# A DLRM tower on one Trainium2 core: the order and the banks of the last round's layers

## Chip, cores and metric

The kernel runs on one core of a Trainium2 (trn2) chip. The metric is the device time of one execution in microseconds; the time of a kernel is the median of its runs.

## What is computed

For each of 2048 batch rows, 26 embedding rows of 128 floats are fetched from 26 tables (1000 to 125000 rows each) by `ids`. Together with the dense vector they are 27 vectors; the 351 products of pairs of them, and the dense vector twice, go through three layers:

```python
combined = jnp.concatenate([dense_features[:, None, :], sparse_features], axis=1)
interactions = jnp.einsum('bnd,bmd->bnm', combined, combined)
interactions_flat = interactions[:, _TRIU_I, _TRIU_J]
z = jnp.concatenate([dense_features, interactions_flat], axis=1)
h = jnp.concatenate([z, r_dense_features], axis=1)
h = jnp.maximum(h @ W_top1 + b_top1, 0.0)      # 607 -> 512
h = jnp.maximum(h @ W_top2 + b_top2, 0.0)      # 512 -> 256
y = h @ W_top3                                 # 256 -> 1
```

All data are 32-bit floats.

## The kernel before

The batch is cut into eight rounds of R = 256 rows. Two rounds are one pass `i`; a round has two tiles of 128 rows, so a pass has tiles v = 0 to 3. The text calls the two rounds of the last pass (r = 0 and 1) its older and its last half.

**Where the vectors come from.** Nine small tables are kept in SBUF in a high and a low part (t_hi, t_lo), and their rows are fetched by products with a one-hot matrix that DVE makes (`fetch`, L477, and `compare`, L763). The other 17 tables are gathered from HBM by POOL, one indirect DMA for each table and tile (`gather_tile`, L402), with a clear of unread memory between two gathers (`pause`, L391). The gathered rows of a tile and its dense rows lie in `rows`, in five groups of 4, 4, 4, 4 and 2. PE transposes a group when its gathers have landed (`transpose_rows`, L437), and ACT and DVE copy the groups by turns into `vecs` (`copy_vecs`, L604).

**Products of pairs.** `dots` (L461) multiplies the vectors of two batch rows with themselves, 32 matmuls for 64 rows and a call; one call fills the two banks of `dots_ps`, the last call of the kernel those of `late_ps` (`last_dots_ps`). ACT copies a part of each block into `inter` (`take_products`, L648, 16 copies), and DVE merges the other part in with a mask (`merge_products`, L811, 16 merges). A tile has two such calls, so 32 copies and 32 merges.

**Input of layer 1.** `x_hi` and `x_lo` hold five slots of 128 inputs: four of products of pairs (JG = 4) and, as the fifth, the dense vector. ACT rounds `vecs` (L653) and `inter` (L657) into x_hi, and DVE subtracts for x_lo (L820, L823). This is `split_input`.

**Layers.** `layer1` (L500) makes M1 = 4 blocks of 128 outputs for the 256 rows of a round, in two banks by turns (mlp_ps[m % 2]). Each block takes 15 products: w_hi by x_hi and w_lo by x_hi for the five slots, then w_hi by x_lo. ACT adds the bias and rectifies a block (`rectify1`, L664), which frees its bank. `layer2` (L509) has M2 = 2 blocks of four products, each issued as two instructions, and starts when all four blocks of layer 1 are rectified. `rectify2` (L671) waits for both blocks. `layer3` (L516) has two products, also two instructions each, and starts when both are rectified. DVE copies the result out (`keep_y`, L831), and SP writes it to HBM (`write_y`, L346).

**The order of the work.** Every engine's order is written out by hand in `step` and `last_step`. In all rounds but the last, layers of one round run between fetches of the next. `last_step(i)` has no next round. On PE it is:

```python
transpose_rows(i, 3, (2,))
layer2(i, 0, 0)
stay_busy(row_ps, 14)
transpose_rows(i, 3, (3,))
layer2(i, 0, 1)
stay_busy(row_ps, 4)
transpose_rows(i, 3, (4,))
dots(i, 3, 0)
dots(i, 3, 1, last_dots_ps)
layer3(i, 0)
stay_busy(turn_ps[1], 20)
layer1(i, 1, *range(M1))      # then layer2(i, 1, 0), layer2(i, 1, 1), layer3(i, 1)
```

`stay_busy(bank, n)` (L523) issues n transposes of the identity into a bank that nobody reads: the unread products. ACT's `last_step` ends with take_products for tile 3, split_input(i, 3), four rectify1 and two rectify2; DVE's with merge_products for tile 3, keep_y(i, 0), split_input(i, 3) and keep_y(i, 1). `turn_ps` are three banks that groups and fetched items use by turns (`taken` tells when a turn's bank has been copied out); its first is the second bank of late_ps.

Of the kernel before, what the change touches and what calls it, by code (L numbers as in the profile page):

```python
# [5 lines left out]
P = 128  # L6
# [12 lines left out]
def dlrm_tower(nc, dense, ids, ids_by_round, tables, w1, w1_laid, w2, small_laid, out):  # L19
# [52 lines left out]
    with ExitStack() as ctx:  # L72
# [81 lines left out]
        mlp_ps = [ps(f"mlp_ps{m}", [P, 512])[:, 0:R] for m in range(2)]  # L154

# [266 lines left out]
        def _(pe):  # L422
# [96 lines left out]

            def stay_busy(bank, n):  # L520

                for _ in range(n):
                    pe.transpose(bank[:, 0:P], ident[:], ident[:])  # L523
# [49 lines left out]
            def last_step(i):  # L573
# [10 lines left out]
                stay_busy(row_ps, 14)  # L584
# [7 lines left out]

                stay_busy(turn_ps[1], 20)
                layer1(i, 1, *range(M1))
                layer2(i, 1, 0)
                layer2(i, 1, 1)
                layer3(i, 1)
# [22 lines left out]
        def _(act):  # L620
# [30 lines left out]
            def split_input(i, v):  # L651
                mine = slice((v % 2) * P, (v % 2 + 1) * P)
                nc.scalar.copy(x_hi[:, JG, mine].rearrange("p (h two s) -> p h two s", two=2, s=QS),  # L653
                               in_turn(vecs[v // 2][:, v % 2, :, 0])).then_inc(x_hi_made, 1)
                act.wait_ge(inter_by_act, i * (4 * NA) + (v + 1) * NA)
                act.wait_ge(inter_by_dve, i * (4 * ND) + (v + 1) * ND)
                nc.scalar.copy(x_hi[:, 0:JG, mine], inter[:]).then_inc(x_hi_made, 1)  # L657
# [69 lines left out]
            def last_step(i):  # L727
# [7 lines left out]
                split_input(i, 2)  # L735
                take_vectors(i, 3, 3)
# [3 lines left out]
                split_input(i, 3)  # L740
                rectify1(i, 1, *range(M1))
                rectify2(i, 1, 0, 1)
# [4 lines left out]
        def _(dve):  # L747
# [68 lines left out]
            def split_input(i, v):  # L816
# [4 lines left out]
                                  ALU.subtract).then_inc(x_lo_made, 1)  # L821
                dve.wait_ge(x_hi_made, i * 8 + v * 2 + 2)
# [3 lines left out]
            def keep_y(i, r):  # L826
# [4 lines left out]
                dve.tensor_copy(in_turn(y_sb[:, r, :]),  # L831
                                mlp_ps[0][0:1].rearrange("p (h two s) -> p h two s", two=2, s=QS)).then_inc(y_kept, 1)
# [52 lines left out]
            def last_step(i):  # L885
# [4 lines left out]
                split_input(i, 2)  # L890
                take_vectors(i, 3, 4)
# [3 lines left out]
                split_input(i, 3)  # L895
                keep_y(i, 1)
# [64 lines left out]
```

## Time and profile before

| | us |
|---|---|
| median of 3 runs | 477.35 (477.17 to 479.39) |
| profiled execution | 478.75 |
| its span, first to last instruction | 477.0 |
| mean granted clock of TensorE, share of full | 0.953 |
| PE busy | 417.5 |
| POOL busy | 399.8 |
| DVE busy | 338.8 |
| ACT busy | 215.8 |

PE is TensorE, PEld its weight loads, DVE VectorE, ACT ScalarE, POOL GpSimd, SP the engine that issues plain DMAs. Busy times overlap, so they don't add up to the span. A granted clock of 1.00 is the upper level of TensorE's clock (2.4 GHz), 0.50 the lower (1.2 GHz). All times in the rows are counted from the start of the span; a start together with a duration and a count (x14) is a run of like instructions that follow one another, the duration that of the whole run. Successive products overlap by their drain, so the end of one lies behind the start of the next.

### The profile page before, as it was taken

Reading aid. Unit: us, or ns where it says so; the run is one execution under the profiler, and the core shown is the slowest. Engines: PE = TensorE matmul, PEld = TensorE weight load, DVE = VectorE, ACT = ScalarE, POOL = GpSimd, SP = SyncE. Lnnn points to the kernel's source line nnn. Section 1 sums busy time; section 2 is a strip of 40 time slices with the busy share of each in tenths; the row PEclk is TensorE's granted clock in tenths of the full one; section 3 lists DMA queues with packets and bytes.
Section 4 is the critical chain, followed back from the end, with each engine's and each line's share of the span. In section 5 each row is a group of like instructions: output and inputs, shape, how many; then the busy total and the mean of one; then the engine's idle time right before and its main releaser. Section 6 shows DMA issues by size and latency. Waiting matters only on the chain.

```text
span 477.0 us, 11689 instructions
## 1 busy us (share of the span) xinstructions
PE 417.5 (88%) x4198; PEld 393.0 (82%) x4198; DVE 338.8 (71%) x777; ACT 215.8 (45%) x719; POOL 399.8 (84%) x553
## 2 busy tenths in 40 slices
PE   0546796979999999999999959999699969999796
PEld 0446696979999999899999959999698969899685
DVE  3659869798598769886897648875587848855060
ACT  1054254454545545545553624554254453545251
POOL 7999989989899898898998989989898988989300
PEclk9958788899999999999999979999899998999899
DMA  7973422622132222123223313222222213131000
GB/s 182 232 199 106 113 51 76 166 70 80 47 84 53 72 73 78 47 74 81 56 64 76 81 39 85 55 78 63 46 78 74 83 39 85 40 78 39 23 2 0
DMA packets 19682, 36.58 MB, mean 77 GB/s; under 512 B 7823, under 2 KB 10391, under 8 KB 19630
## 3 DMA queue, kind: packets, MB, share of 16 engines
q0 software_dynamic: 8704, 17.84, 16.6%
q1 hardware_dynamic: 10926, 18.04, 13.0%
q8 instruction: 33, 0.54, 0.5%
q14 instruction: 19, 0.16, 0.1%
HBM read 35.85 MB, written 0.01 MB: 75 GB/s over the span
## 4 chain that ended last, share of the span: by engine, by line
POOL 64%; issue 27%; PE 4%; ACT 2%; POOLq 1%; DMA 1%; DVE 0%; ACTq 0%; DVEq 0%
POOL rows L402 36%; POOL y_wide L391 28%; PE mlp_ps L500 2%; PE mlp_ps L509 1%; ACT inter L648 1%; POOLq L390 1%; DMA rows<-in_tbl,idx_sb 1%; PE dots_ps L461 0%; DVE inter L811 0%; DMA idx_sb<-in_ids 0%; PE mlp_ps L516 0%; PE late_ps L437 0%; ACT x_hi L657 0%; ACT h_sb L664 0%; ACT h_sb L671 0%
## 5 line engine op out<-in xcount | busy, mean ns | idle before, releaser
L402 POOL DMA_INDIRECT rows<-in_tbl,idx_sb x272 | 265.8, 977 | 45.6 <-POOL y_wide L391 43.8
L763 DVE TENSOR_TENSOR onehot<-ids_sb,late_ps 125x1024 fp32r<-125x1024 int32 (+2 forms) x154 | 167.8, 1142 | 12.6 <-DMA ids_sb<-in_ids_by_round 6.4
L811 DVE COPY_PREDICATED inter<-mask,dots_ps 27x48 f32<-27x48 int32 x496 | 103.1, 208 | 60.4 <-ACT inter L648 45.7
L391 POOL MEMSET y_wide<- 64x448 f32 x272 | 133.8, 492 | 0.2
L648 ACT COPY inter<-dots_ps 27x64 f32<-27x64 f32 x496 | 99.0, 200 | 59.1 <-PE dots_ps L461 47.8
L461 PE MATMUL dots_ps<-vecs 128*64 128x54 f32 x1984 | 118.7, 226 | 1.5 <-ACT vecs L624 0.9
L461 PEld LDWEIGHTS dots_ps<-vecs 128*64 128x64 f32 x1984 | 114.7, 140 | 6.0 <-issue 2.4
L477 PE MATMUL turn_ps<-onehot,t_hi 125*128 125x256 f32 x378 | 101.1, 304 | 10.3 <-DVE vecs L604 10.3
L477 PE MATMUL turn_ps<-onehot,t_lo 125*128 125x256 f32 x378 | 96.5, 291 | 0.0
L477 PEld LDWEIGHTS turn_ps<-onehot,t_hi 125*128 125x128 f32 x378 | 75.8, 200 | 14.8 <-issue 8.5
L477 PE MATMUL late_ps<-onehot,t_hi 125*128 125x256 f32 x214 | 59.7, 312 | 21.1 <-DVE t_lo L776 16.6
L477 PEld LDWEIGHTS turn_ps<-onehot,t_lo 125*128 125x128 f32 x378 | 76.0, 201 | 0.2
L477 PEld LDWEIGHTS late_ps<-onehot,t_hi 125*128 125x128 f32 x214 | 44.5, 208 | 24.4 <-DVE t_lo L776 18.8
L624 ACT COPY vecs<-turn_ps 128x256 f32<-128x256 f32 x46 | 28.2, 613 | 71.0 <-PE turn_ps L477 69.8
L477 PE MATMUL late_ps<-onehot,t_lo 125*128 125x256 f32 x214 | 56.5, 298 | 0.0
L477 PEld LDWEIGHTS late_ps<-onehot,t_lo 125*128 125x128 f32 x214 | 44.5, 208 | 0.1
L437 PE MATMUL turn_ps<-ident,rows 128*128 128x128 f32 x200 | 30.5, 282 | 13.3 <-DMA rows<-in_tbl,idx_sb 7.6
L500 PE MATMUL mlp_ps<-x_hi,w_hi 128*128 128x256 f32 x160 | 41.0, 291 | 1.2 <-ACT x_hi L657 1.2
L500 PE MATMUL mlp_ps<-x_hi,w_lo 128*128 128x256 f32 x160 | 39.6, 282 | 0.0
L604 DVE COPY vecs<-turn_ps 128x512 f32<-128x512 f32 (+1 forms) x28 | 17.9, 639 | 30.0 <-PE turn_ps L437 29.9
L437 PEld LDWEIGHTS turn_ps<-ident,rows 128*128 128x128 f32 x200 | 22.7, 143 | 15.9 <-DMA rows<-in_tbl,idx_sb 9.1
L624 ACT COPY vecs<-late_ps 128x256 f32<-128x256 f32 x26 | 16.0, 616 | 38.5 <-PE late_ps L477 38.0
(52 smaller groups left out, 353.3 us busy)
## 6 DMA issues: line engine op xcount, KB each, us to landing
ids_sb<-in_ids_by_round SPq DMA_DIRECT2D x25, 375.0 KB
rows<-in_tbl,idx_sb POOLq DMA_INDIRECT x272, 2.6
vecs<-in_tbl SPq DMA_DIRECT2D x8, 448.0 KB
rows<-in_r_dense_features SPq DMA_DIRECT2D x16, 64.0 KB, 5.2
h_sb<-in_W_top_laid SPq DMA_DIRECT2D x2, 512.0 KB, 18.3
vecs<-in_tbl SPq DMA_DIRECT2D x1, 560.0 KB
w_sb<-in_W_top SPq DMA_DIRECT2D x1, 512.0 KB
vecs<-in_tbl SPq DMA_DIRECT2D x8, 52.0 KB
```

What stands on the lines that cost most here:

```text
L390: pool.sem_inc(pauses_begun, 1)
L391: pool.memset(unread, 0.0).then_inc(pauses_made, 1)
L402: nc.gpsimd.indirect_dma_start(out=rows[v % 2][:, s, :], out_offset=None, in_=tables[f - 1][:, :], in_offset=bass.IndirectOffsetOnAxis(ap= ...
L437: last = pe.transpose(bank[:, n * P:(n + 1) * P], rows[u][:, s, :], ident[:])
L461: last = pe.matmul(place[h * 64:h * 64 + 64, n, 0:PAIR], vs[:, b:b + 2, :].rearrange("p b f -> p (b f)"), vs[:, b:b + 2, 0:N], start=True, ...
L477: last = pe.matmul(bank, part[0:KP, T0[k] + t, :], part_buffer(k, h)[0:KP, t - a, :], start=(t == 0 and part is t_hi), stop=(t == KT[k] - ...
L500: last = pe.matmul(mlp_ps[m % 2], w[:, jj, m * P:(m + 1) * P], x[:, jj, :], start=(at == 0), stop=(at == 3 * (JG + 1) - 1))
L604: copy(vecs[v // 2][:, v % 2, :, a:a + n], bank_of("rows", i * 4 + v, k)[:, 0:n * P].rearrange("p (f b) -> p b f", f=n)).then_inc(done, 1)
L624: nc.scalar.copy(vecs[(r + 1) % 2][:, :, :, NR + k], bank_of("item", i * 2 + r + 1, k)[:, 0:R].rearrange("p (t b) -> p t b", t=2)).then_in ...
L648: nc.scalar.copy(inter_of(u, q, g, 0, count[g]), products_of(q, g * JG, count[g], place)).then_inc(inter_by_act, 1)
L763: dve.tensor_tensor(part_buffer(k, h)[0:KP, 0:n], home.rearrange("p (o r) -> p o r", o=1).to_broadcast([KP, n, R]), row_of[KT[k]][0:KP, a: ...
L811: dve.copy_predicated(inter_of(u, q, g, a, n), mask[g * 32:g * 32 + N, a:a + n].rearrange("p (j s) -> p j s", s=1).to_broadcast([N, n, QS] ...
```

## The change

The last round's end is rewritten; all other rounds stay as they are.

- PE, ahead of the fourth group of tile 3: 32 unread products for 14.
- ACT and DVE: `split_input` is cut in two. The part for the dense vector of tile 3 (`split_dense`) is issued right after the split of tile 2, on ACT behind a wait for the copy of that tile's first group; the part for the products of pairs stays where it was.
- PE: `end_of_layers` takes the place of the 20 unread products, layer1, layer2 and layer3 of the last half. Layer 1 has a bank for each of its four blocks: two of turn_ps and the two of dots_ps, which are free once the merges of the first call of tile 3 are done. The three dense products of each block come first, then 14 unread products, then the 12 others of each block.
- PE, layer 2: first the products of both blocks with the first three parts of h1, then those with the fourth. Each product waits for its own ReLU. Each block reports by itself.
- ACT: each block of layer 2 is rectified when it is done, into another buffer (in `rows`). Layer 3's products wait for one block each, and its result goes into the first of the four banks.

```diff
+        flat_dots_ps = dots_ps[:].rearrange("p s c -> p (s c)")
+        end_ps = [turn_ps[1][:, 0:R], turn_ps[2][:, 0:R], flat_dots_ps[:, 0:R], flat_dots_ps[:, 512:512 + R]]
+        end_h2_sb = rows[0][:, 0:M2 * R // D, :].rearrange("p s d -> p (s d)").rearrange("p (m r) -> p m r", r=R)
...
+            def end_of_layers(i):
+                parts, before = i * 8 + 8, i * (2 * M1) + M1
+                pe.wait_ge(x_hi_made, parts - 1)
+                pe.wait_ge(x_lo_made, parts - 1)
+                pe.wait_ge(inter_by_act, i * (4 * NA) + 3 * NA + PER_UNIT)
+                pe.wait_ge(inter_by_dve, i * (4 * ND) + 3 * ND + PER_UNIT)
+                for m in range(M1):
+                    for n, (w, x) in enumerate(((w_hi, x_hi), (w_lo, x_hi), (w_hi, x_lo))):
+                        pe.matmul(end_ps[m], w[:, JG, m * P:(m + 1) * P], x[:, JG, :], start=(n == 0), stop=False)
+                stay_busy(mlp_ps[1], 14)
+                for m in range(M1):
+                    for at in range(3 * JG):
+                        if at < 2 * JG:
+                            jj, w, x = at // 2, (w_hi, w_lo)[at % 2], x_hi
+                        else:
+                            jj, w, x = at - 2 * JG, w_hi, x_lo
+                        if m == 0 and at == 0:
+                            pe.wait_ge(x_hi_made, parts)
+                        if m == 0 and at == 2 * JG:
+                            pe.wait_ge(x_lo_made, parts)
+                        last = pe.matmul(end_ps[m], w[:, jj, m * P:(m + 1) * P], x[:, jj, :],
+                                         start=False, stop=(at == 3 * JG - 1))
+                    last.then_inc(h1_done, 1)
+                pe.wait_ge(y_kept, i * 2 + 1)
+                for ks in (range(M1 - 1), (M1 - 1,)):
+                    for m in range(M2):
+                        for k in ks:
+                            pe.wait_ge(relu1_done, before + k + 1)
+                            last = pe.matmul(mlp_ps[m], w2_sb[:, k, m * P:(m + 1) * P], h1_sb[:, k, :],
+                                             start=(k == 0), stop=(k == M1 - 1))
+                        if M1 - 1 in ks:
+                            last.then_inc(h2_done, 1)
+                for k in range(M2):
+                    pe.wait_ge(relu2_done, i * (2 * M2) + M2 + k + 1)
+                    last = pe.matmul(end_ps[0][0:1], w3_sb[:, k:k + 1], end_h2_sb[:, k, :],
+                                     start=(k == 0), stop=(k == M2 - 1))
+                last.then_inc(y_done, 1)
...
-                stay_busy(row_ps, 14)
+                stay_busy(row_ps, 32)
...
-                stay_busy(turn_ps[1], 20)
-                layer1(i, 1, *range(M1))
-                layer2(i, 1, 0)
-                layer2(i, 1, 1)
-                layer3(i, 1)
+                end_of_layers(i)
...
                 split_input(i, 2)
+
+                act.wait_ge(*taken(turn_of["rows", i * 4 + 3, 0]))
+                split_dense(i, 3)
                 take_vectors(i, 3, 3)
                 rectify2(i, 0, 0, 1)
                 take_products(i, 3, 0)
                 take_products(i, 3, 1, last_dots_ps)
-                split_input(i, 3)
-                rectify1(i, 1, *range(M1))
-                rectify2(i, 1, 0, 1)
+                split_input(i, 3, False)
+                for m in range(M1):
+                    act.wait_ge(h1_done, i * (2 * M1) + M1 + m + 1)
+                    nc.scalar.activation(h1_sb[:, m, :], end_ps[m], ACT.Relu, bias=b1_sb[:, m:m + 1]).then_inc(relu1_done, 1)
+                for m in range(M2):
+                    act.wait_ge(h2_done, i * (2 * M2) + M2 + m + 1)
+                    nc.scalar.activation(end_h2_sb[:, m, :], mlp_ps[m], ACT.Relu,
+                                         bias=b2_sb[:, m:m + 1]).then_inc(relu2_done, 1)
...
                 split_input(i, 2)
+                split_dense(i, 3)
                 take_vectors(i, 3, 4)
                 merge_products(i, 3, 0)
                 merge_products(i, 3, 1, last_dots_ps)
                 keep_y(i, 0)
-                split_input(i, 3)
-                keep_y(i, 1)
+                split_input(i, 3, False)
+                keep_y(i, 1, end_ps[0])
```

## Rows read from the trace of the kernel before

**Rows 1.** The page: busy time by engine, and the chain that ended last.

```profile
PE 417.5 (88%) x4198; PEld 393.0 (82%) x4198; DVE 338.8 (71%) x777; ACT 215.8 (45%) x719; POOL 399.8 (84%) x553
...
POOL 64%; issue 27%; PE 4%; ACT 2%; POOLq 1%; DMA 1%; DVE 0%; ACTq 0%; DVEq 0%
```

**Rows 2.** Chain of waits near its end: start, us, what.

```profile
441.70 2.56 DMA rows<-in_tbl,idx_sb
```

**Rows 3.** PE's timeline: start, us, line, operation, count, [idle before <-releaser].

```profile
438.32 1.89 PE L509 MATMUL mlp_ps<-h_sb,w_sb 128*128 128x256 f32 x8
440.05 1.69 PE L523 MATMUL late_ps<-ident 128*128 128x128 f32 x14
444.31 0.97 PE L437 MATMUL late_ps<-ident,rows 128*128 128x128 f32 x4 [2.57 <-DMA rows<-in_tbl,idx_sb]
445.08 3.30 PE L509 MATMUL mlp_ps<-h_sb,w_sb 128*128 128x256 f32 x8
...
448.65 0.38 PE L437 MATMUL turn_ps<-ident,rows 128*128 128x128 f32 x2
...
457.56 2.40 PE L523 MATMUL turn_ps<-ident 128*128 128x128 f32 x20
461.15 0.35 PE L500 MATMUL mlp_ps<-x_hi,w_hi 128*128 128x256 f32 x1 [1.18 <-ACT x_hi L657]
...
467.81 0.76 PE L500 MATMUL mlp_ps<-x_lo,w_hi 128*128 128x256 f32 x5
469.23 3.69 PE L509 MATMUL mlp_ps<-h_sb,w_sb 128*128 128x256 f32 x16 [0.66 <-ACT h_sb L664]
473.85 1.02 PE L516 MATMUL mlp_ps<-h_sb,small 128*1 128x256 f32 x4 [0.93 <-ACT h_sb L671]
```

**Rows 4.** POOL's last gather (start, us); landing times of gathers, 438 to 450 us.

```profile
444.92 0.95 POOL L402 DMA_INDIRECT rows<-in_tbl,idx_sb  x1 [0.16 <-POOL y_wide L391]
...
DMA to landing us min/median/max: 2.5/2.5/2.6
```

**Rows 5.** Busy by engine; last three columns: granted clock, DMA share, GB/s.

```profile
440.00:444.31 4.31, 1.74 (x15) 1.45 (x14) 0.23 (x1) 0.00 (x0) 3.90 (x6) 1.00 0.17 46
444.31:448.00 3.69, 3.69 (x12) 3.12 (x13) 0.00 (x0) 0.59 (x1) 1.88 (x3) 0.54 0.14 36
457.56:461.15 3.59, 2.41 (x22) 2.20 (x21) 3.18 (x15) 2.22 (x8) 0.00 (x0) 1.00 0.00 0
```

**Rows 6.** ACT's timeline.

```profile
445.32 0.59 ACT L604 COPY vecs<-late_ps 128x512 f32<-128x512 f32 x1 [6.45 <-PE late_ps L437]
...
458.89 0.42 ACT L653 CAST x_hi<-vecs 128x128 fp32r<-128x128 f32 x1
460.43 0.62 ACT L657 CAST x_hi<-inter 128x512 fp32r<-128x512 f32 x1 [1.12 <-DVE inter L811]
...
468.61 0.47 ACT L664 ACTIVATE h_sb<-mlp_ps,small 128x256 f32<-128x256 f32 x1 [1.32 <-PE mlp_ps L500]
472.96 0.84 ACT L671 ACTIVATE h_sb<-mlp_ps,small 128x256 f32<-128x256 f32 x2 [3.88 <-PE mlp_ps L509]
```

**Rows 7.** DVE's timeline.

```profile
449.07 0.42 DVE L604 COPY vecs<-turn_ps 128x256 f32<-128x256 f32 x1 [8.84 <-PE turn_ps L437]
...
456.55 3.79 DVE L811 COPY_PREDICATED inter<-mask,late_ps 27x48 f32<-27x48 int32 x16
460.37 0.41 DVE L831 COPY y_wide<-mlp_ps 1x256 f32<-1x256 f32 x1
...
461.10 0.68 DVE L823 TENSOR_TENSOR x_lo<-inter,x_hi 128x512 fp32r<-128x512 f32 x1
```

**Rows 8.** 64 small products on PE, early and late; 56 to 62.4 us as rows 5.

```profile
58.99 5.16 PE L461 MATMUL dots_ps<-vecs 128*64 128x54 f32 x64 [0.90 <-ACT vecs L624]
...
430.96 3.75 PE L461 MATMUL dots_ps<-vecs 128*64 128x54 f32 x64
...
56.00:62.40 6.40, 5.50 (x47) 5.24 (x47) 4.01 (x4) 1.91 (x2) 5.75 (x9) 0.51 0.33 97
```

More of the change, by code:

```diff
@@ L154, in dlrm_tower @@
         mlp_ps = [ps(f"mlp_ps{m}", [P, 512])[:, 0:R] for m in range(2)]
+        flat_dots_ps = dots_ps[:].rearrange("p s c -> p (s c)")
+        end_ps = [turn_ps[1][:, 0:R], turn_ps[2][:, 0:R], flat_dots_ps[:, 0:R], flat_dots_ps[:, 512:512 + R]]
+        assert M1 == len(end_ps)
+        end_h2_sb = rows[0][:, 0:M2 * R // D, :].rearrange("p s d -> p (s d)").rearrange("p (m r) -> p m r", r=R)
         ident_set = sem("ident_set")
@@ L649, in take_products, with split_dense @@
                                        products_of(q, g * JG, count[g], place)).then_inc(inter_by_act, 1)
-            def split_input(i, v):
+            def split_dense(i, v):
                 mine = slice((v % 2) * P, (v % 2 + 1) * P)
@@ L654, in split_input @@
                                in_turn(vecs[v // 2][:, v % 2, :, 0])).then_inc(x_hi_made, 1)
+            def split_input(i, v, dense_too=True):
+                mine = slice((v % 2) * P, (v % 2 + 1) * P)
+                if dense_too:
+                    split_dense(i, v)
                 act.wait_ge(inter_by_act, i * (4 * NA) + (v + 1) * NA)
@@ L814, in merge_products, with split_dense @@
                             products_of(q, c + SECOND, n, place)).then_inc(inter_by_dve, 1)
-            def split_input(i, v):
+            def split_dense(i, v):
                 mine = slice((v % 2) * P, (v % 2 + 1) * P)
@@ L821, in split_input @@
                                   ALU.subtract).then_inc(x_lo_made, 1)
+            def split_input(i, v, dense_too=True):
+                mine = slice((v % 2) * P, (v % 2 + 1) * P)
+                if dense_too:
+                    split_dense(i, v)
                 dve.wait_ge(x_hi_made, i * 8 + v * 2 + 2)
@@ L824, in split_input, with keep_y @@
                                   ALU.subtract).then_inc(x_lo_made, 1)
-            def keep_y(i, r):
+            def keep_y(i, r, bank=mlp_ps[0]):
                 dve.wait_ge(y_done, i * 2 + r + 1)
@@ L831, in keep_y @@
                 dve.tensor_copy(in_turn(y_sb[:, r, :]),
-                                mlp_ps[0][0:1].rearrange("p (h two s) -> p h two s", two=2, s=QS)).then_inc(y_kept, 1)
+                                bank[0:1].rearrange("p (h two s) -> p h two s", two=2, s=QS)).then_inc(y_kept, 1)
             def step(now, prev):
```

## The prediction

> **What bounds the kernel now.** I read the page's shares and chain first, then the chain of waits from 430 us on, then the timelines of PE, ACT and DVE over the same stretch, and the granted clock in chosen windows. PE is busy 88% of the span and POOL 84%, yet the chain that ended last is 64% POOL: its gathers and the clears between them set the pace of everything up to the last rows [rows 1]. The change touches only what comes after, so the pace of POOL stays as it is, and the question is what the stretch from 440 us to the end is made of.
>
> That stretch has three pieces. First the last two groups of rows. The fourth group of the last tile lands at 441.70 + 2.56 = 444.26 us and is transposed at 444.31; behind it PE runs one block of layer 2 of the older half, 3.30 us, and only then the fifth group, at 448.65 [rows 2, 3]. But the last gather was issued at 444.92 and gathers take 2.5 to 2.6 us to land [rows 4]: its rows were there at about 447.52, and PE was 1.13 us late for them. It was late because of the clock. The eight products of layer 2 take 3.30 us there and 1.89 us at 438.32 [rows 3]; the mean granted clock of 444.31 to 448.00 is 0.54 of full, which is the lower level (1.2 GHz) for nearly all of it, against 1.00 up to 444.31 [rows 5]. Before the fall PE had idled 2.57 us behind 14 unread products.
>
> Second, the products and their merging, 449.59 to 461.05: 128 small products, 32 copies by ACT, 32 merges by DVE, and the cast x_hi at 460.43. DVE's last 16 merges begin at 456.55 and end at 460.34, and the cast starts at once behind them [rows 6, 7]. PE waits here; the change leaves the length of this piece alone.
>
> Third, the last half's layers on PE: 60 products of layer 1 from 461.15 to 468.57, 0.66 us idle for the last ReLU, 16 instructions of layer 2 (eight products of two each) for 3.69 us, 0.93 us idle for the two ReLUs, and 1.02 us of layer 3 [rows 3]. PE is the bound wherever it isn't waiting for ACT.
>
> **The change, part by part.**
>
> *32 unread products for 14.* Six more cost 2.40 - 1.69 = 0.71 us (20 against 14), 0.118 us each [rows 3]; 18 more end at 440.05 + 1.69 + 18 x 0.118 = 443.86 us. The rows land at 444.27, so nothing waits for them, with 0.4 us to spare, and PE's idle stretch falls from 2.57 to some 0.45 us. What does this do to the clock? No row shows 32 of them, so both ends: nothing (the fall comes as before), or no fall. The nearest row is 457.56 to 461.15: 20 unread products and then 1.18 us of idle, and the clock stays at 1.00 through it and behind it [rows 5]. I take no fall. Then layer 2 starts at about 444.8 and needs 1.89 us, the four unread products 0.45 more: PE is through at about 447.2, before the rows at 447.52. The fifth group is transposed at 447.52 in place of 448.65: **1.13 us**, and DVE's copy (449.07), the products and all that follows come as much earlier. DVE waits there for PE [rows 7], and ACT's ReLUs of that half are done by 447.6 (446.7 + 0.04 + 0.84), ahead of its next work. The upper end is also 1.13, since the gather sets it; the lower is 0.
>
> The Trainium skill says otherwise ("TensorE: Matmul & The Clock Gate", Part 4: PE-mode transpose): work in transpose mode does not count as PE activity for the clock, and the unread products are transposes. By that rule the 18 added ones would buy nothing. The row of 457.56 to 461.15 speaks against it, but that stretch is shorter than the 4.31 us before the fall, so the rule stays as a rival below.
>
> *The dense part moved.* ACT's cast of the dense vector (0.42 us at 458.89) and DVE's subtraction move from behind the last merges to the gap in which ACT idles 6.45 us and DVE 8.84 us [rows 6, 7]. Both are issued there right after the split of tile 2, their input was copied by DVE ahead of that, and ACT's needs 0.42 us of its gap and DVE's, over as many elements, about as much. Without that cover the cost would be 0.4 us on the copy of the fourth group. Leaving the old place brings nothing by itself: the cast stood in ACT's wait for the merges, the subtraction between keep_y at 460.37 and 461.10, in DVE's wait for x_hi. PE's 12 dense products (four banks by three) now run behind layer 3 of the older half, where 20 unread products stood. They wait for the merges out of dots_ps, over at 456.5, before PE comes at 457.56. One product of layer 1 costs (467.81 - 461.15) / 55 = 0.121 us [rows 3], so 12 cost 1.45; with 14 unread ones (1.69) PE is done at 457.56 + 3.14 = 460.70 on the old time axis, 0.45 us before x_hi lets it go on. What remains behind the wait is 48 products for 60: **1.45 us**. The low part x_lo is wanted after eight products, at 461.15 + 0.97 = 462.12 in place of 462.41; DVE has it at 461.10 + 0.68 = 461.78 [rows 7]. Still in time, by 0.3 us less a semaphore's step. No queue of DMAs is passed by anything here; the write of the first y keeps its place.
>
> *Layers 2 and 3 half by half.* The first six of the eight products of layer 2 need only the first three ReLUs. The third one is issued 1.45 us before layer 1 ends and takes 0.47 us [rows 6], so PE goes on without a gap. That removes the 0.66 us idle and adds back the overlap of streams: the row at 438.32 ends at 440.21 while the next begins at 440.05, 0.16 us. Together **0.82 us**. The last two products (0.44 us each, 3.69 us being eight of them and the drain) want the fourth ReLU 2.6 us later; it needs 0.04 + 0.47 + 0.14. Behind layer 2, which ends at T: before, ACT starts at T + 0.04, two ReLUs take 0.84, PE starts 0.05 later and takes 1.02, in all 1.95 us. After: the first ReLU runs from T - 0.40 to T + 0.07, and the first product of layer 3 from T + 0.12 to T + 0.56; the second ReLU runs from T + 0.04 to T + 0.51, and the second product starts at T + 0.56 and takes 1.02 - 0.44 = 0.58. In all 1.14 us: **0.81 us**.
>
> *Added waits.* Layer 2 gets eight waits and layer 3 two where there was one each, nearly all on what is long done. The nearest row is PE's start 0.05 us behind the second ReLU [rows 3, 6]; the bounds are 0 and 10 x 0.05 = 0.5 us. I take 0, since PE takes the waits while the product before them runs. Behind each of them is only the rest of the layers. The new banks (turn_ps, dots_ps) are read by nobody while PE writes them. No gain is possible from either.
>
> **The sum.** 1.13 + 1.45 + 0.82 + 0.81 = 4.21 us. The profiled execution took 478.75 us (span 477.0 and 1.75 around it): 474.5 for its like. The median of the runs shown is 1.40 below it, 477.35, and 477.35 - 4.21 = 473.1; with 0.1 for the waits, **473.2 us**. A measurement of this kernel can tell a change of about 0.5%, 2.4 us, from none.
>
> **The rivals.**
> (A) The forecast, chance 0.58: all four terms, 472.4 to 474.0.
> (B) The front gives little or nothing, 0.28: the clock falls in spite of the unread products, or the unprofiled runs fell at a moment where layer 2 was spared, so that there was less to win. Then 3.08 us remain, 474.3 (bounds 473.8 to 475.0). For it: the fall is an event of one execution, and no row shows a stretch of over 2.4 us of unread products. Against it: the stretch at 457.56. If the Trainium skill's sentence on transposes holds here, this case is the outcome, with the clock again low from about 444.5.
> (C) The tail yields less than half, 0.10: waits inside layer 2 that cost more than the 0.05 us each, or x_lo late by some tenths. Under 2.4 us in all: 475.0 to 477.0.
> (D) Slower, 0.04, one mechanism: the clock falls in the last 25 us, over the products and layer 1, since the unread products ahead of x_hi go from 20 to 14. Each microsecond at the lower level costs half of one where PE is the bound; 64 small products took 5.16 us at the low clock against 3.75 at the full one [rows 8]. It decides from 8.4 us at the lower level on. A stretch nearly that long is in this trace: 56.0 to 62.4 us has a mean of 0.51 [rows 8]. With 10 us low it ends at 478.2, 13 us 479.7. Against it: PE idles only 0.45 us there in place of 1.18, and 12 true products stand where unread ones did.
>
> **How the numbers follow.** A and B hold 0.86. The range takes A's lower bound with a little for the spread of medians and reaches to the upper bound of B: 472.2 to 475.2. Faster by over 0.5% is under 474.96: nearly all of A, most of B, 0.83. Within 0.5%: the rest of B, C and the milder half of D, 0.15. Slower: 0.02, D where it lasts over 13 us.
>
> **What the profile after would show.** Right: 32 unread products ending about 0.4 us before the fourth group's transposes; clock 1.00 there; layer 2's eight instructions in 1.9 us; the fifth group's transposes directly behind the landing of the last gather; 12 products before x_hi and 48 after; layer 2 directly behind layer 1; some 1.1 us from its end to the end of layer 3. From the start of the cast x_hi to the end of layer 3: 14.4 us before, 11.4 after. Wrong: layer 2 still taking 3.3 us (B), gaps inside layer 2 or behind the eighth product of layer 1 (C), a granted clock under 1.00 after 449 us (D).

## The result, and the profile after

The changed kernel takes 475.31 us (median of 22 runs, 472.03 to 477.55) against 477.52 us of the kernel before (22 runs): ratio 0.9956, 95% interval 0.9939 to 0.9974, or 2.1 us gained. The forecast was 4.2 us gained and 473.2 us; the result lies 0.1 us above the upper end of the range. Three later measurements of the same kernel, on three different chips, gave ratios of 0.9934, 0.9936 and 0.9929 (below), so 2.1 to 3.4 us in all. Half to four fifths of the forecast gain is there.

The profiled execution of the changed kernel took 477.40 us, span 475.4. Its PE timeline, from the end of tile 2 on (columns as in [rows 3]; L570 is the unread products, L515 and L557 layer 2, L548 the new layer 1, L563 layer 3):

```profile
422.37 0.44 PE L443 MATMUL turn_ps<-ident,rows 128*128 128x128 f32 x2 [1.93 <-DMA rows<-in_tbl,idx_sb]
...
442.06 1.97 PE L515 MATMUL mlp_ps<-h_sb,w_sb 128*128 128x256 f32 x8 [1.57 <-ACT h_sb L711]
443.86 3.66 PE L570 MATMUL late_ps<-ident 128*128 128x128 f32 x32
447.35 0.60 PE L443 MATMUL late_ps<-ident,rows 128*128 128x128 f32 x4
447.79 1.89 PE L515 MATMUL mlp_ps<-h_sb,w_sb 128*128 128x256 f32 x8
449.52 0.60 PE L570 MATMUL late_ps<-ident 128*128 128x128 f32 x4
449.95 0.38 PE L443 MATMUL turn_ps<-ident,rows 128*128 128x128 f32 x2
...
460.39 1.69 PE L570 MATMUL mlp_ps<-ident 128*128 128x128 f32 x14
462.60 0.39 PE L548 MATMUL turn_ps<-x_hi,w_hi 128*128 128x256 f32 x1 [0.52 <-ACT x_hi L704]
...
468.47 3.62 PE L557 MATMUL mlp_ps<-h_sb,w_sb 128*128 128x256 f32 x16
472.22 1.02 PE L563 MATMUL turn_ps<-rows,small 128*1 128x256 f32 x4
```

The tail (everything behind the wait for x_hi) is nearly as forecast. Layer 2 starts at 468.47, before layer 1's last product has drained, and layer 3 ends at 473.24. From the cast x_hi (461.93) to there are 11.3 us; before, 14.4 [rows 3, 6]; forecast 11.4.

The front (the stretch of the unread products and the last two groups) is not. In [rows 3] PE began the unread products at 440.05 and then idled for the rows. Here it begins them at 443.86, 3.8 us later, while POOL's last gather is issued at nearly the same time:

```profile
445.07 0.95 POOL L408 DMA_INDIRECT rows<-in_tbl,idx_sb  x1 [0.16 <-POOL y_wide L397]
```

There is no idle time before the fourth group now; the rows had landed at about 444.2 (that group's last gather, issued at 441.57, and 2.6), and PE was still busy with unread products until 447.35. The fifth group comes at 449.95, 4.88 us behind the last gather's issue; it was 3.73 before and forecast as 2.60.

PE came late for two reasons. First, it idled 1.93 us for tile 2's fifth group, and then the clock fell, over layer 1 and the products of pairs of tile 2. The busy time by engine of that stretch (columns as in [rows 5]; granted clock 0.50):

```profile
423.90:427.10 3.20, 3.20 (x25) 2.98 (x25) 0.00 (x0) 0.47 (x1) 2.88 (x4) 0.50 0.16 41
```

Second, ACT stood still between its 8th and 9th copy out of the second products, and again before the last ReLU of the older half's layer 1, for which PE waited 1.57 us. ACT's timeline:

```profile
435.81 1.75 ACT L690 COPY inter<-dots_ps 27x64 f32<-27x64 f32 x8 [1.74 <-PE dots_ps L467]
438.30 1.78 ACT L690 COPY inter<-dots_ps 27x64 f32<-27x64 f32 x8 [0.74 <-PE dots_ps L467]
440.10 0.58 ACT L646 COPY vecs<-turn_ps 128x512 f32<-128x512 f32 x1
441.44 0.47 ACT L711 ACTIVATE h_sb<-mlp_ps,small 128x256 f32<-128x256 f32 x1 [0.75 <-PE mlp_ps L506]
```

The profile names PE as releaser, but PE's last product of that call had ended at 437.23, ahead of the eighth copy's end (437.56). In the kernel before the 16 copies were one run of 3.56 us. None of this is code that the change touches. Whether the change makes such lateness more frequent all the same is taken up under e1 to e4.

### The profile page after: what moved, and what is told of

It reads as the page before. It is cut to its first block, busy times and chain, and to the rows that moved or that the text cites. A ratio compares the mean times of both kernels' runs of the same rounds, so it can differ in the third digit from the quotient of the medians.

```text
span 475.4 us, 11713 instructions
## 1 busy us (share of the span) xinstructions
PE 416.0 (87%) x4210; PEld 391.8 (82%) x4210; DVE 337.1 (71%) x777; ACT 214.8 (45%) x719; POOL 399.9 (84%) x553
## 4 chain that ended last, share of the span: by engine, by line
POOL 61%; issue 25%; PE 8%; DMA 1%; POOLq 1%; DVE 1%; ACT 1%; DVEq 0%; ACTq 0%
POOL rows L408 34%; POOL y_wide L397 27%; PE dots_ps L467 2%; PE mlp_ps L506 2%; DMA rows<-in_tbl,idx_sb 1%; DVE inter L866 1%; POOLq L396 1%; PE late_ps L570 1%; PE mlp_ps L515 1%; PE turn_ps L548 1%; PE mlp_ps L557 1%; PE dots_ps L548 1%; ACT inter L690 1%; DMA idx_sb<-in_ids 0%; PE turn_ps L443 0%
## 5 line engine op out<-in xcount | busy, mean ns | idle before, releaser
L483 PE MATMUL turn_ps<-onehot,t_hi 125*128 125x256 f32 x378 | 100.5, 302 | 11.4 <-DVE vecs L646 11.4
L506 PE MATMUL mlp_ps<-x_hi,w_hi 128*128 128x256 f32 x140 | 35.9, 291 | 0.0
L506 PE MATMUL mlp_ps<-x_hi,w_lo 128*128 128x256 f32 x140 | 34.7, 283 | 0.0
```

The source lines that it names most:

```text
L483: last = pe.matmul(bank, part[0:KP, T0[k] + t, :], part_buffer(k, h)[0:KP, t - a, :], start=(t == 0 and part is t_hi), stop=(t == KT[k] - ...
L506: last = pe.matmul(mlp_ps[m % 2], w[:, jj, m * P:(m + 1) * P], x[:, jj, :], start=(at == 0), stop=(at == 3 * (JG + 1) - 1))
```

## The experiments

In the tables below, A is the start of the unread products ahead of tile 3's fourth group, L the issue of the last gather, both of the one profiled execution; "fifth" is the start of the fifth group's transposes less L, "rest" the time from there to the end of layer 3. Ratios are to the kernel before on the same chip; e1 to e4 ran on one chip, e5 to e8 on another, e9 to e12, e13 to e16, and e17 and e18 on three more. Medians in us are best compared within such a group; L itself, which neither part of the change can reach, lies between 442.70 (e18) and 445.34 us (e2), and that scatter is in every time.

| kernel | unread | A - L | fifth | rest | ratio (95% interval) | median, before's |
|---|---|---|---|---|---|---|
| before | 14 | -4.87 | 3.73 | 26.22 | | |
| changed, first | 32 | -1.21 | 4.88 | 23.29 | 0.9956 (0.9939 to 0.9974) | 475.31, 477.52 |
| e1 new tail | 14 | -5.05 | 3.67 | 23.29 | 0.9936 (0.9912 to 0.9960) | 474.56, 477.80 |
| e2 old tail | 32 | -4.71 | 2.51 | 26.26 | 0.9979 (0.9960 to 0.9997) | 477.03, 477.80 |
| e3 new tail | 64 | -4.90 | 4.69 | 23.28 | 0.9964 (0.9947 to 0.9981) | 476.23, 477.80 |
| e4 new tail | 0 | | 3.58 | 23.33 | 0.9961 (0.9943 to 0.9978) | 475.30, 477.80 |
| e5 changed | 32 | -3.96 | 2.54 | 23.35 | 0.9934 (0.9917 to 0.9952) | 474.70, 477.83 |
| e6 8 more at tile 2 | 32 | -4.88 | 2.55 | 23.34 | 0.9923 (0.9910 to 0.9936) | 474.17, 477.83 |
| e7 other order | 10 | | 2.58 | 23.38 | 0.9950 (0.9932 to 0.9969) | 475.61, 477.83 |
| e8 no last comparison | 32 | -4.94 | 2.53 | 23.13 | 0.9919 (0.9906 to 0.9932) | 474.35, 477.83 |
| e9 PE delayed | 32 | -1.62 | 4.48 | 23.27 | 0.9984 (0.9962 to 1.0006) | 476.24, 477.76 |
| e10 PE delayed | 14 | -1.08 | 3.05 | 23.29 | 0.9946 (0.9923 to 0.9969) | 475.33, 477.76 |
| e11 e6 and e8 | 32 | -2.55 | 3.54 | 23.08 | 0.9934 (0.9913 to 0.9956) | 474.58, 477.76 |
| e12 changed | 32 | -0.17 | 5.92 | 23.29 | 0.9936 (0.9915 to 0.9958) | 474.92, 477.76 |
| e13 no ninth round | 32 | -4.87 | 2.71 | 23.13 | 0.9914 (0.9886 to 0.9941) | 474.10, 478.39 |
| e14 that, 8 at tile 2 | 26 | -5.00 | 2.58 | 23.12 | 0.9901 (0.9877 to 0.9925) | 473.89, 478.39 |
| e15 changed | 32 | -3.89 | 2.59 | 23.35 | 0.9929 (0.9906 to 0.9953) | 475.00, 478.39 |
| e16 as e1 | 14 | -4.28 | 2.60 | 23.36 | 0.9915 (0.9891 to 0.9940) | 474.34, 478.39 |
| e17 as e14 | 14 | -2.09 | 2.45 | 23.13 | 0.9939 (0.9916 to 0.9961) | 473.86, 477.60 |
| e18 as e14 | 26 | -2.84 | 2.65 | 23.12 | 0.9936 (0.9910 to 0.9961) | 474.19, 477.60 |

### e1 to e4: the parts alone, and the number of unread products

e1, e3 and e4 are the changed kernel with another number; e2 is the kernel before with 32. The expectations weigh three explanations: theory O (overrun: PE comes late in some executions, and 32 unread products then outlast the landing), rival T (the tail itself yields less), and rival C, also called theory C (the held clock gives its 1.13 us in most executions).

```diff
# e1: 14, e3: 64, e4: the line left out
-                stay_busy(row_ps, 32)
+                stay_busy(row_ps, 14)
# e2, in the kernel before
-                stay_busy(row_ps, 14)
+                stay_busy(row_ps, 32)
```

> The changed kernel with 14 unread products ahead of the fourth group, as before, in place of 32; the tail is the new one. Theory O (overrun): PE reaches the unread products at a moment that differs by microseconds from run to run (440.05 us in the trace of before, 443.86 in that of after), the gathers do not, so 32 of them (3.5 us) outlast the landing wherever PE is late; the tail brings its 3.1 us always. Then this kernel beats the changed one by about 1 us: ratio to before about 0.9935, 474.4 us for a before of 477.5. Rival T (the tail brings only 2.1 us outside the one profile, 32 products cost nothing): 0.9956, the same as the changed kernel. Rival C (the clock held by 32 products brings its 1.13 us in most runs): slower than the changed kernel by 1 us, 0.998. In the profile: PE's transposes of the fifth group start within 0.3 us of the last gather's issue plus 2.6 us, or, where the clock falls, up to 1.3 us behind it.

> The kernel before with 32 unread products in place of 14 and nothing else of the change. Theory O: slower than before by about 1 us, ratio 1.002, with a wider spread of the runs (early arrivals of PE gain up to 1.1 us, late ones lose up to 2). Rival T: 1.000. Rival C: 0.9976 (1.13 us gained).

> The changed kernel with 64 unread products: they end behind the landing in every run, so PE sets the start of the products of pairs. Theory O: 32 more at 0.11 us are 3.5 us more wherever 32 already overran; median about 2.5 to 3.5 us above the changed kernel, ratio to before about 1.002; and the spread of the runs becomes that of PE's arrival. Rival T: little change up to some 0.9990. By the Trainium skill (TensorE: Matmul & The Clock Gate, Part 4: PE-mode transpose) transposes do not count as activity: then the granted clock falls to 0.50 during these 7 us, and the eight products of layer 2 behind them take 3.3 us in place of 1.9. If they count, the clock is 1.00 from the first of them to the fifth group's transposes.

> The changed kernel without any unread product ahead of the fourth group (the four ahead of the fifth stay). Theory O: no overrun at all, but PE idles up to 4.3 us there in early runs and the clock falls in more of them, each worth up to 1.3 us; about as fast as with 14: ratio 0.993 to 0.995. Rival C: the slowest of these but for 64, 0.998 or more. In the profile: clock 0.50 in layer 2 behind the fourth group where PE came early, 1.00 where it came late.

The tail alone (e1) came out at 0.9936, as expected (0.9935). The front alone (e2) was 0.9979 (0.9960 to 0.9997): a gain of 1.0 us, where theory O expected a loss of 1 and C 0.9976. Its profile is the one forecast, gathers as the bound and the clock kept:

```profile
440.63 3.66 PE L523 MATMUL late_ps<-ident 128*128 128x128 f32 x32
444.73 0.66 PE L437 MATMUL late_ps<-ident,rows 128*128 128x128 f32 x4 [0.45 <-DMA rows<-in_tbl,idx_sb]
445.23 1.89 PE L509 MATMUL mlp_ps<-h_sb,w_sb 128*128 128x256 f32 x8
446.96 0.60 PE L523 MATMUL late_ps<-ident 128*128 128x128 f32 x4
447.85 0.44 PE L437 MATMUL turn_ps<-ident,rows 128*128 128x128 f32 x2 [0.29 <-DMA rows<-in_tbl,idx_sb]
```

So each part alone does about what was forecast, and rival T falls, since the tail alone brings 3.1 us; C fits e2 but not e1 (0.998 expected, above e1's interval). The two gains add up to 4.1 us, the forecast, but the changed kernel, which has both, gave 2.1 to 3.4. Theory O missed e2 in the spread as well: it expected a wider one, and the 12 runs lie within 1.6 us, where the first 22 of the changed kernel span 5.5. Neither profile with the old tail shows PE late. So it isn't excluded that the new tail, though it stands behind the place, makes a late PE more frequent; no run tests that.

With 64 the products outlast the landing though PE is in time: fifth at 4.69. The median lies 1.7 us above e1's, and by the ratios 1.3 to 1.7 us above the three later measurements of the changed kernel (expected 2.5 to 3.5). Without any (e4) PE idles 4.26 us and the clock falls as in [rows 5]; the ratio, 0.9961, is outside the expected 0.993 to 0.995, though its interval reaches in.

e3 also shows what unread products do to the clock. By engine, its 64 and what follows:

```profile
439.60:446.59 6.99, 6.99 (x65) 6.99 (x64) 0.50 (x2) 0.00 (x0) 5.85 (x8) 1.00 0.15 40
446.59:449.00 2.41, 2.41 (x17) 2.15 (x16) 0.00 (x0) 0.63 (x2) 0.00 (x0) 1.00 0.00 0
```

Seven microseconds of nothing but transposes, granted clock 1.00 in them and behind them. By the Trainium skill ("TensorE: Matmul & The Clock Gate", Part 4: PE-mode transpose) they would not hold it up; the trace does not agree.

### e5 and e12: the changed kernel again

> The changed kernel itself once more. Its first profile showed PE at the 32 unread products only 1.2 us before the last gather's issue; the four kernels run since showed 4.7 to 5.2 us. Theory L (a late PE in some runs): the last gather of tile 2 landed 3.2 us after its issue instead of about 2.1, PE idled 1.93 us for it, the clock fell at 423.9 and PE came 3.7 us late; in runs where that doesn't happen the fifth group starts 2.5 us after the last gather's issue, and the run ends near 473. So: runs in two groups, one of 472 to 474, one of 476 to 477.5, median 474 to 475.3; ratio to before 0.992 to 0.9955. If this profile is of the early kind: unread products from about 4.9 us before the last gather's issue, fifth group 2.5 us after it. Rival S (the change makes PE late in every run): this profile again 1 to 2 us before the issue.

> The changed kernel a third time, beside the others on one chip. If PE's lateness differs from run to run: ratio between the two measured so far, 0.9934 and 0.9956. In the profile, late kind (unread products from 1 to 3 us before the last gather's issue, fifth group over 3 us behind it) or early kind (4 to 5 us, 2.54), as the first two times; a third reading of either tells only how often.

The two profiles are of the two kinds, early and late. e5 took 473.98 us and has all that was forecast: 32 products from 440.04, fifth 2.54 behind the last issue. e12 took 477.89 us and is later still than the first: PE idled 2.14 us at tile 2, the clock fell between 423 and 424, ACT stood still 1.45 us between its copies, and the unread products begin at 444.62. Of the 41 runs of the changed kernel (four times, e15 among them) 11 are above 476.2 us; of the 13 with 14 products (e1, e16) none is above 475.5. The two separate groups of runs that e5's expectation names are not there: the six runs are spread evenly from 473.4 to 476.2 us. Rival S (the change makes PE late in every execution) falls with e5.

Where the clock doesn't fall behind the fourth group, the profiles with 32 products fit one rule: the fifth group starts at the later of L + 2.55 (landing) and A + 6.09 (PE's work from the first of 32 unread products). A + 6.09 is 449.95 in the first profile (measured 449.95), 450.71 in e12 (450.71), 447.75 in e11 (447.75), 448.52 in e9 (448.53); for e5 it is 446.13, the landing 446.55, measured 446.54. The largest miss is 0.16 us (e13, landing bound: L + 2.71). For 64 products the one profile gives A + 9.59, 449.19 in e3.

### e6, e7, e8: against the fall at tile 2

```diff
# e6
-                transpose_rows(i, 2, range(NG))
+                transpose_rows(i, 2, range(NG - 1))
+                stay_busy(mlp_ps[1], 8)
+                transpose_rows(i, 2, (NG - 1,))
# e7: e6 and
                 layer2(i, 0, 0)
-                stay_busy(row_ps, 32)
+                layer2(i, 0, 1)
+                stay_busy(row_ps, 10)
                 transpose_rows(i, 3, (3,))
-                layer2(i, 0, 1)
-                stay_busy(row_ps, 4)
+                stay_busy(row_ps, 12)
# e8, DVE's last step before last_step
-                compare(i, r, 9)
+                if not (static(i) and i == PASSES - 1 and r == 0):
+                    compare(i, r, 9)
```

> The changed kernel with 8 more unread products (0.9 us) between the fourth and the fifth group of tile 2, where PE idled 1.93 us before the clock fell. Theory L: the clock no longer falls there, PE is in time in nearly all runs, the upper group of runs disappears, median about 473.3: ratio to before 0.991 to 0.9925. Rival S: no change against the changed kernel. Against the forecast of theory L it would be if the median stays within 0.5 us of the changed kernel's.

> As the run before, and in place of 32 unread products ahead of the fourth group and a block of layer 2 between the groups: both blocks of layer 2 and 10 unread products ahead of the fourth group, 12 between fourth and fifth. From PE's arrival to the fifth group 1.7 + 2.5 + 0.5 = 4.7 us in place of 6.1, so a PE that is up to 2.4 us late costs nothing, where 32 products allow 1.3. Theory L: as fast as the run before where PE is in time, faster where it is late: median equal or up to 0.7 us lower. If the clock falls in the 1.5 us of idle that stay on either side, the products of pairs are slower by up to 1 us, and this kernel is slower than the run before.

> The changed kernel without two loads of ids (375 KB each) and one comparison that prepare a ninth round, which does not exist. One of the loads is issued 2.2 to 3.3 us before the last gather of tile 2 and shares the DMA engines with it. Theory L, with this load as the cause of the late landing: the gather lands 2.1 to 2.6 us after its issue in every run, PE idles under 1 us, the clock stays, and the median falls to about 473.3, ratio 0.991 to 0.9925, with runs within 2.5 us of each other. If the load is not the cause, the ratio stays that of the changed kernel.

Theory L says that a late landing at tile 2 and the fall behind it are what makes PE late. It expected a median of 473.3 for both; they came out at 474.17 and 474.35, 0.5 and 0.35 us below e5, with runs within 1.4 us of each other, and their intervals overlap e5's. By e6's own sign (within 0.5 us of the changed kernel speaks against L) this is on the edge: theory L is neither shown nor refuted by them. e8 did not do what its expectation says: SP runs its steps in a loop, where the condition on a fixed `i` never holds, so both loads stayed and only the comparison (a ninth round's, two instructions of DVE) went. e7 is slower than e6 by 1.4 us in the median, though its profile (473.53 us, the fastest of its six runs) shows the intended order, a full clock and 1.27 us of idle on both sides. Four of its runs are above 475.3. That the clock falls over the products in those is the expectation's guess; no profile caught one.

### e9 and e10: PE late on purpose

```diff
                 dots(i, 2, 1)
+                stay_busy(row_ps, 24)
# e10 also
-                stay_busy(row_ps, 32)
+                stay_busy(row_ps, 14)
```

> The changed kernel with 24 more unread products (2.7 us) on PE behind the products of pairs of tile 2, so that PE comes some 2.2 us late to the 32 ones in every run; otherwise the same. Overrun by lateness: from the first of the 32 to the fifth group PE needs 6.1 us (profiles of the changed kernel), so a PE that starts them 2.6 us before the last gather's issue starts the fifth group 3.3 to 3.5 us behind it, where the changed kernel's second profile shows 2.54: 0.8 to 1.0 us slower than the changed kernel in its early runs, ratio to before 0.994 to 0.997. If lateness of PE is not what costs, the ratio stays at 0.9934.

> The same lateness with 14 unread products: PE needs 4.1 us from the first of them to the fifth group and is ready before the gather lands, and idles 0.5 us instead of 2.7 before the fourth group, so the clock stays up. Fifth group 2.5 to 2.6 us behind the last gather's issue, as in the early runs of the changed kernel: ratio 0.991 to 0.9925, 0.8 to 1 us faster than with 32. If what the 32 products give were their own (and not the short idle stretch), this kernel would show 3.7 us and a ratio of 0.994.

This is the test of the overrun. With PE late, the fifth group starts at 4.48 with 32 and 3.05 with 14; from A it is 6.10 and 4.13 us, 1.97 less. The medians are 0.9 us apart in the same direction (1.8 by the ratios, whose intervals touch), so the profiles carry this reading and the times agree with it. Both kernels were slower than expected (0.9984 for 0.994 to 0.997, 0.9946 for 0.991 to 0.9925): PE was later than planned (A - L of -1.62 and -1.08 for -2.6), and bound even with 14. From 440 to 450 us the clock is 1.00 in both. So the value of the 18 products changes sign with A. In time they gain 1.13 us where 14 would end in a fall (fifth 3.67 in e1, 2.54 in e5) and nothing where they would not (2.60 in e16); where PE is the bound they cost 18 x 0.11 = 2.0 us.

### e11, e13, e14: what makes PE late

```diff
# e11: e6 and e8 together
# e13: e8, with SP's steps written out, so that its two loads go
+                wanted = not (static(i) and i == PASSES - 1 and r == 0)
+                if wanted: load_ids(i, r, 3)     # and load_ids(i, r, 4)
-            passes(sp, step, last_step)
+            written_out(step, last_step)
# e14: e13 and e6's 8 products, and 26 for 32
```

> The changed kernel with the 8 unread products ahead of tile 2's fifth group and without the loads of ids and the comparison for a ninth round. PE in time in every run: ratio 0.991 to 0.992 and runs within 2 us of each other. If lateness has another source, its spread is that of the changed kernel (over 3 us) and its ratio above 0.993.

> The changed kernel without the last two loads of ids and the comparison for a ninth round; this time SP's steps are written out, so that the loads really go (in the two kernels named quiet they stayed, and only the comparison went, since SP runs its steps in a loop). The load issued 2.2 to 3.2 us before the last gather of tile 2 is gone. If it is what makes that gather land 2.7 to 3.6 us after its issue in the late profiles (2.1 to 2.6 in the others): landing at 2.0 to 2.2 us here, PE idle there under 0.8 us, clock 1.00 from 418 us on, unread products begun 4.5 us or more before the last gather's issue, fifth group 2.55 us behind it, ratio 0.990 to 0.992. If the load has no part in it: landing and ratio as the changed kernel's.

> The same, with 8 unread products ahead of tile 2's fifth group and 26 in place of 32 ahead of tile 3's fourth. From the first of the 26 to the fifth group PE needs 6.09 - 6 x 0.112 = 5.4 us, so it may begin up to 2.9 us before the last gather's issue at no cost (3.55 with 32); in time it idles 1.1 us before the fourth group, about what the stretch at 457 us of the kernel before showed without a fall. Ratio 0.990 to 0.992, and no run above 475.5. If the clock falls in that idle stretch: fifth group 3.2 us or more behind the issue, and 0.993.

The expectations counted the gathers of a tile as 16; they are 17, so the last gather of tile 2 is the one before. Counted rightly, the load of 375 KB is issued 0.1 to 1.6 us ahead of it. In the profiles with that load PE's transposes of the fifth group start 3.7 to 5.4 us behind the gather's issue; 5.06 in the first profile of the changed kernel and 5.41 in e12, where the load came 0.37 and 0.38 us ahead. The first of these two, SP's load and POOL's gather (PE's start at 422.37 is shown above):

```profile
416.94 0.28 SPq L306 DMA_DIRECT2D ids_sb<-in_ids_by_round  x1
...
417.31 1.18 POOL L408 DMA_INDIRECT rows<-in_tbl,idx_sb  x1 [0.16 <-POOL y_wide L397]
```

In tile 3, with no load about, gathers land after 2.5 to 2.6 us [rows 4]. In e13 the rows were there when PE came, 3.1 us behind the issue at the latest (the last two of the six):

```profile
416.87 0.95 POOL L411 DMA_INDIRECT rows<-in_tbl,idx_sb  x1 [0.16 <-POOL y_wide L400]
...
419.48 0.90 PE L446 MATMUL turn_ps<-ident,rows 128*128 128x128 f32 x6
```

In none of the four profiles without the load (e13, e14, e17, e18) does PE wait there or the clock fall there. But e14, e17 and e18 also have e6's 8 products, and with these PE hardly waits there with the load either (e6, e7 and e11: 0.25 us at most). So one profile, e13, speaks for the load as the first source of lateness; it is likely, not shown.

It isn't the second. e11's expectation said what another source would look like, a ratio above 0.993 and a spread of over 3 us, and so it came: 0.9934 and 3.1 us. In e11, e17 and e18 PE is late (A - L of -2.55, -2.09, -2.84) with no fall at tile 2, and ACT stands still for 0.74 to 1.46 us between the 8th and 9th copy, as in the first profile and in e12. In e17 a fall is part of it too, behind the wait for ACT's ReLU and ahead of the unread products: the eight products of layer 2 take 3.45 us for the usual 1.9.

```profile
436.55 0.66 PE L446 MATMUL turn_ps<-ident,rows 128*128 128x128 f32 x4 [0.51 <-DMA rows<-in_tbl,idx_sb]
438.52 3.45 PE L518 MATMUL mlp_ps<-h_sb,w_sb 128*128 128x256 f32 x8 [1.32 <-issue]
441.77 1.94 PE L573 MATMUL late_ps<-ident 128*128 128x128 f32 x14
```

The seven profiles with A - L above -3 (two of them delayed on purpose) all have this standstill, of 0.74 us or more; of the others (A - L of -3.89 and below, and e4 and e7) one has 0.43 us there (e14) and the rest none. It is always between the same two copies. Nothing that the profile shows releases it, and what it is stays open. e13 and e14 came out inside their expected ratios (0.9914 and 0.9901); e14's is the lowest of all.

### e15 to e18: what the added products are worth

> The changed kernel beside the one with 14 products (next run) on one chip: what the 18 more products are worth in the median. In time they gain 1.15 us, late they cost 1.96 us; with a third of the runs late both kernels lie within 0.4 us of each other. Were all runs in time, this one would be 1.1 us faster.

> The changed kernel with 14 unread products once more, beside the changed kernel: ratio to before 0.9935 as the first time, and the two within 0.4 us (a third of the runs late) or 1.1 us slower (none late).

> As e14 (no load of ids for a ninth round, 8 unread products at tile 2), with 14 unread products ahead of tile 3's fourth group in place of 26. With PE in time in every run the short row of 14 leaves 2.5 us of idle there, the clock falls in most runs and the fifth group starts 3.6 us behind the last gather's issue: 1.1 us slower than with 26, ratio to before 0.992 to 0.993. (The profile of the second kernel with 14 showed 1.99 us of idle and no fall, so the fall may stay away in some runs; then the two lie within 0.6 us.) The load named in earlier expectations was issued ahead of the gather before the one they count from, 0.1 to 1.6 us ahead of tile 2's true last gather.

> The same kernel as e14, beside the one with 14: ratio to before 0.989 to 0.992, fifth group 2.55 to 2.6 us behind the last gather's issue, no run above 475.5 for a before of 477.8.

Side by side, 32 products (e15, 0.9929) and 14 (e16, 0.9915) are not told apart, the 14 ahead by 0.7 us in the medians (expected: within 0.4 us, or 1.1 behind). With e1 (0.9936) beside e5 and e12 (0.9934, 0.9936), the 18 products bring nothing in the median. e16's profile shows one more thing: after 14 unread products PE idled 1.99 us and the clock did not fall, so that even in time there was nothing to win:

```profile
440.09 1.69 PE L570 MATMUL late_ps<-ident 128*128 128x128 f32 x14
443.77 0.66 PE L443 MATMUL late_ps<-ident,rows 128*128 128x128 f32 x4 [1.99 <-DMA rows<-in_tbl,idx_sb]
444.26 1.89 PE L515 MATMUL mlp_ps<-h_sb,w_sb 128*128 128x256 f32 x8
...
446.97 0.44 PE L443 MATMUL turn_ps<-ident,rows 128*128 128x128 f32 x2 [0.38 <-DMA rows<-in_tbl,idx_sb]
```

e17 and e18 are equal too (medians 0.3 us apart); the expected 1.1 us between 14 and 26 is not there, and both ratios, 0.9939 and 0.9936, lie above what was expected (0.992 to 0.993, 0.989 to 0.992). e18 repeats e14 with 0.9936 for 0.9901, the intervals overlapping. The 12 runs of e14's kernel together have a median of 474.1 and none above 474.8, against 475.2 and 477.9 for the 41 of the changed kernel. That it beats the kernel before is shown; that it beats the changed one is likely, not shown, since the runs come from different chips.

## Why the prediction was wrong, point by point

**The tail: right in mechanism, 0.15 to 0.2 us off in size.** Forecast 1.45 + 0.82 + 0.81 = 3.08. Measured, fifth group to end of layer 3: 26.22 before and 26.26 in e2, 23.27 to 23.38 in the kernels with the new tail and all comparisons, that is 2.9 us. The three terms themselves are there: cast to end 3.1 us shorter, layer 2 without a gap, layer 3 ending 1.15 us behind layer 2 (472.09 to 473.24; forecast 1.14). Against them stands a stop of 0.24 us in DVE's merges, ahead of the cast, which the kernel before doesn't have:

```profile
457.08 0.95 DVE L866 COPY_PREDICATED inter<-mask,dots_ps 27x48 f32<-27x48 int32 x4 [0.24 <-issue]
```

In e8, with two DVE instructions fewer ahead of it, the stop is gone and the rest is 23.13:

```profile
451.72 3.78 DVE L869 COPY_PREDICATED inter<-mask,dots_ps 27x48 f32<-27x48 int32 x16 [3.24 <-ACT inter L693]
```

The stop is in all 12 profiles with the new tail and the comparison and in none of the 6 without the comparison, where the rest is 23.08 to 23.13, a gain of 3.1 us as forecast. So it seems to hang on where in DVE's stream the merges stand. The change shifts them by moving the dense subtraction ahead of them, a move that the prediction put at no cost; that this is what brings the stop is argued, since no run moves the subtraction alone. The other added waits cost nothing that shows; the sum took them at 0 and then added 0.1 us for them.

**The front: the step that failed** is "18 more end at 443.86 us. The rows land at 444.27, so nothing waits for them, with 0.4 us to spare". It took PE's arrival of one execution as given. Gathers keep their pace by POOL's own clears; PE does not keep its own against them. Its arrival moves by 4.9 us over the profiles (A - L from -0.17 to -5.05). By the working above 32 products are free only if PE begins them 3.54 us or more before L (6.09 - 2.55), 14 if it is 1.5 us or more. Where PE is in time, all was as written: fifth 2.51 to 2.59 (forecast 2.60), clock 1.00, layer 2 in 1.89 us (e2, e5, e15). Where it is late, the products are 2.0 us of work in front of the path.

**The bounds.** "The upper end is also 1.13; the lower is 0" left out that an added stretch of work can cost its whole length. Rival D looked for the slower case in the clock at the end, where no profile shows a fall; the true one, unread products that overrun when PE is late, wasn't among the rivals. By its number alone, 475.31 lies in C's band (475.0 to 477.0), but C's mechanism is not there: no waits inside layer 2, no late x_lo, and a tail that gave 2.9 us. Rival B ("the front gives little or nothing", 474.3) is the nearest to what was measured, through another mechanism: not a fall in spite of the products, but gain in some executions and loss in others. Its second half, executions in which the clock spared layer 2 anyway, is e16's. How much of the missing 0.8 to 2.1 us each of these (late PE, spared clock) takes stays open: the unprofiled runs can't be sorted, and e1 and e2, added, miss nothing.

**The clock** was weighed rightly on the one point on which B's first half rested: 64 transposes in a row kept it at 1.00 in e3. No profile with 32 of them and PE in time shows a fall behind them (e2, e5, e6, e8, e13, e15).

**The numbers.** Case A at 0.58 was too sure for a step with 0.4 us of slack read from one execution, on a kernel whose own runs shown then differed by 2.2 us.

## What to carry to other kernels

A filler that keeps an engine busy until data lands is real work when the engine is late: size it by the latest arrival seen in several executions, not by the idle time of one, and put a price on the overrun. Slack of a fraction of a microsecond between two engines that keep separate paces is no slack. Work taken off a chain behind the last join (dense products ahead of the wait, halves of a layer that start on their own inputs) paid in each of the 18 profiles that have it: whichever of gather and PE comes first ahead of it, its length stays within 0.3 us.

## What the runs showed of the hardware

- The same idle length had both outcomes for the clock: it fell behind 1.32 us of idle (e17) and 1.93 us (changed kernel, tile 2), and did not behind 1.74 us (e11), 1.75 us (e18) and 1.99 us (e16). 14 unread products and 2.57 us of idle ended in a fall [rows 3, 5].
- Where a plain load of 375 KB was issued 0.1 to 0.4 us ahead of a gather, PE's work on the gathered rows began 4.6 to 5.4 us behind the gather's issue (six profiles); with the load 1.2 to 1.6 us ahead, 3.7 to 4.2 us. Without the load the one free profile (e13) had the rows within 3.1 us, and gathers of tile 3 landed within 2.6.
- ACT can stand still for 0.74 to 1.46 us at a wait whose producer ended earlier, in the same program in one execution (e12, 1.45 us) and not in another (e5). Not explained.
- A stop of 0.24 to 0.26 us sits between two merges in DVE's stream of instructions and is gone from there with two instructions fewer ahead of it. Not explained.
